# Group normalisation and a two-way column scan on one core: input loaded in channel blocks, statistics in five batches, the first scan slot split, part of the normalising on GpSimd

## The reference

```python
def ref(feature, conv_w, conv_b, prelu_a):
    Wc = conv_w[:, :, 0, 4]                      # 512 x 512
    def step(prev, x_i):
        y = einsum('oc,nch->noh', Wc, prev) + conv_b
        y = where(y >= 0, y, prelu_a * y)
        cur = y + x_i
        return (cur, cur)
    x = moveaxis(feature, 3, 0)
    _, fwd_rest = scan(step, x[0], x[1:])
    fl = concatenate([x[0:1], fwd_rest])
    _, bwd_rest = scan(step, fl[-1], fl[:-1], reverse=True)
    return moveaxis(concatenate([bwd_rest, fl[-1:]]), 0, 3)

x = x + ref(group_norm(x, G=32, eps=1e-5), ...)
```

## Time and profile before

| | before |
|---|---|
| median of 3 executions | 389.98 us |
| profiled execution, its span | 390.33 us, 388.6 us |
| TensorE busy in the span | 352.3 us (91%) |
| VectorE, ScalarE, GpSimd busy | 295.7, 224.3, 5.1 us |
| mean granted TensorE clock | 0.996 |
| HBM read, written | 13.63 MB, 12.58 MB |

### The profile page before, as it was taken

One profiled execution on the slowest core, in us unless ns is written; L12 is line 12 of the kernel. 1 busy time (PEld: TensorE's weight loads), 2 busy tenths in 40 slices (PEclk: granted clock), 3 DMA queues, 4 the chain that ended last, 5 costly groups with the idle time before them and its releaser, 6 DMA issues.

```text
span 388.6 us, 10101 instructions
## 1 busy us (share of the span) xinstructions
PE 352.3 (91%) x3080; PEld 351.0 (90%) x3080; DVE 295.7 (76%) x963; ACT 224.3 (58%) x799; POOL 5.1 (1%) x11
## 2 busy tenths in 40 slices
PE   0117799999999999999999999999999999999994
PEld 0117799999999999999999999999999999999994
DVE  2899599999765666566566788878888888888785
ACT  2663066566466566556656655665665566556554
POOL 1011100000000000000000000000000000000000
PEclk9999899999999999999999999999999999999999
DMA  7997000000000000000000112222221222222222
GB/s 248 428 422 307 2 0 1 0 0 1 0 0 0 0 0 0 0 0 0 0 0 0 56 54 81 81 69 66 81 81 55 80 81 72 63 81 81 59 76 82
DMA packets 28231, 26.30 MB, mean 68 GB/s; under 512 B 1344, under 2 KB 25920, under 8 KB 26816
## 3 DMA queue, kind: packets, MB, share of 16 engines
q1 hardware_dynamic: 27936, 26.22, 19.9%
q10 hardware_dynamic: 288, 0.00, 0.0%
HBM read 13.63 MB, written 12.58 MB: 67 GB/s over the span
## 4 chain that ended last, share of the span: by engine, by line
PE 73%; DVE 14%; DMA 6%; issue 4%; SPq 1%; ACT 1%; POOLq 0%; POOL 0%; DVEq 0%
PE psum L196 73%; DVE state L284 6%; DMA xio<-in_x 6%; DVE state L328 4%; DVE state L323 2%; DVE bstat L254 1%; SPq L158 1%; ACT above L237 0%; POOLq L41 0%; POOL rstd L387 0%; DVE xio L340 0%; ACT below L239 0%; DVE chan L264 0%; DVEq L105 0%; DVE var_eps L281 0%
## 5 line engine op out<-in xcount | busy, mean ns | idle before, releaser
L196 PE MATMUL psum<-state,w_t 128*128 (+1 forms) x3008 | 339.3, 276 | 2.8 <-DVE state L284 2.4
L196 PEld LDWEIGHTS psum<-state,w_t 128*128 128x128 f32 x3008 | 338.5, 193 | 3.4 <-DVE state L284 2.5
L237 ACT ACTIVATE above<-psum,bias 128x128 f32<-128x128 f32 x376 | 139.9, 372 | 144.4 <-PE psum L196 144.4
L323 DVE TENSOR_TENSOR state<-above,state 128x128 f32 (+1 forms) x376 | 107.5, 288 | 68.5 <-ACT above L237 66.8
L239 ACT ACTIVATE below<-psum,neg_bias 128x128 f32<-128x128 f32 x376 | 140.2, 373 | 0.0
L328 DVE SCALAR_TENSOR_TENSOR state<-below,neg_slope,state 128x128 f32 (+1 forms) x376 | 123.4, 349 | 6.7
L340 DVE TENSOR_TENSOR xio<-xio,state (+1 forms) x48 | 33.2, 692 | 1.7
L284 DVE TENSOR_SCALAR state<-xio,mean,rstd 128x352 f32<-128x352 f32 (+3 forms) x84 | 30.9, 434 | 1.2 <-POOL rstd L387 1.2
L254 DVE BATCH_NORM_STATS2 bstat<-xio 128x6 f32<-128x512 f32 (+2 forms) x45 | 23.6, 584 | 8.5 <-DMA xio<-in_x 8.4
L176 PE MATMUL psum<-chan,same_group 128*128 128x4 f32 x8 | 2.0, 322 | 25.1 <-DVE chan L264 25.1
L176 PEld LDWEIGHTS psum<-chan,same_group 128*128 128x128 f32 x8 | 1.8, 280 | 25.3 <-issue 14.7
(11 more groups left out here) (17 smaller groups left out, 8.3 us busy)
## 6 DMA issues: line engine op xcount, KB each, us to landing
out_y<-xio SPq DMA_DIRECT2D x48, 256.0 KB, 2.6
xio<-in_x SPq DMA_DIRECT2D x11, 1024.0 KB, 16.2
w_t<-in_w SPq DMA_DIRECT2D x4, 256.0 KB, 19.2
xio<-in_x SPq DMA_DIRECT2D x1, 512.0 KB, 26.4
xio<-in_x SPq DMA_DIRECT2D x2, 256.0 KB, 23.5
bias<-in_bias ACTq DMA_DIRECT2D x1, 2.0 KB, 5.1
slope<-in_slope ACTq DMA_DIRECT2D x1, 0.5 KB, 8.6
```

The lines of the kernel that those rows point to most:

```text
L196: mm = nc.tensor.matmul(psum[:, 4 * par + o, 0:COLS], w_t[:, k, o * P:(o + 1) * P], xs[k], start=k == 0, stop=k == 3)
L237: nc.scalar.activation(above[:, par, o, :], z, ACT.Relu, bias=bias[:, o:o + 1], scale=1.0).then_inc(above_done, 1)
L323: nc.vector.tensor_tensor(sts[o], above[:, par, o, :], sts[o], ALU.add).then_inc(part_done, 1)
```

## The change

- **Input and statistics.** The input is laid out and loaded as 16 blocks b = 4k + n of one channel tile and one image (`xin`, 768 KB, 6 KB in a row for each partition); block 0 comes as three pieces and block 15 as 16, 16, 8, 4 and 4 columns, so there are 22 loads. Statistics are per block, with one of three 16-column units on ScalarE in 12 of the blocks. The batches are now tile 0, tile 1, tile 2, tile 3 for images 0 to 2, and tile 3 for image 3.
- **Slot 0** is taken out of the loop and split: its four k = 0 units (`FIRST_A`) stand between the last batch's mean and its second variance matmul, the other 12 (`FIRST_B`) behind it. Each of tiles 0 to 2 waits only for GpSimd's early steps, tile 3 for `first_done`. Tile 0 is now complete after the seventh unit of `FIRST_B`. There are 12 warm-up matmuls instead of 24, once block 14 has come, and the means of the fourth batch stand behind these.
- **Normalising.** For tiles 0 to 2 the first 8 columns are done by GpSimd in chunks of 4 columns (512 elements), a subtraction and a multiplication each. VectorE does tile 3 (image by image) and later pieces of 10 columns: 2 ahead, and 2 after each of slots 0 to 30, which are unrolled.
- **Output.** `add_input` adds the input into the state in place, without its wait; column 0 has its input added before the backward half. Columns 47 to 1 are stored from the state (256 KB, 2 KB in a row for each partition), and column 0 in four stores of 64 KB, one for each tile, which stand on SyncE's queue behind the store of column 1.
- Bias and slope come in one load and are negated in one instruction.

```diff
-PIECES = [[16, 16, 16], [16, 16, 16], [16, 16, 16], [16, 16, 8, 4, 4]]
-EARLY = 4
-LATER = 11
-AHEAD = 8
-PER_STEP = 4
-WARM_UP = 24
+FIRST_A = [(0, 0), (0, 1), (0, 2), (0, 3)]
+FIRST_B = [(1, 0), (1, 1), (1, 2), (1, 3), (2, 0), (2, 1), (3, 0), (3, 1), (2, 2), (3, 2), (2, 3), (3, 3)]
+FIRST_PIECES = [16, 16, 16]
+LAST_PIECES = [16, 16, 8, 4, 4]
+BATCHES = [(0, 0, 4), (1, 0, 4), (2, 0, 4), (3, 0, 3), (3, 3, 4)]
+EARLY = 8
+CHUNK = 4
+LATER = 10
+PER_STEP = 2
+WARM_UP = 12
...
-            for i in range(W):
+            for i in range(FWD):
                 step = W - 1 - i
                 sp.wait_ge(out_ready, i + 1)
-                sp.dma_start(out[:, :, step, :, :], xio[:, :, step, :, :]).then_inc(stored, 16)
-            sp.wait_ge(stored, 16 * W)
+                sp.dma_start(out[step], state[:, step, :, :]).then_inc(stored, 16)
+            for o in range(KT):
+                sp.wait_ge(state_ready, 4 * (STEPS - 1) + o + 1)
+                sp.dma_start(out[0, :, o, :], state[:, 0, o, :]).then_inc(stored, 16)
+            sp.wait_ge(stored, 16 * (FWD + KT))
...
+            for t in range(len(BATCHES) - 1):
+                if t == len(BATCHES) - 2:
+                    pe.wait_ge(x_loaded[NBLK - 2][0], 16)
                     for _ in range(WARM_UP):
                         nc.tensor.matmul(psum[:, 5, 0:P], same_group[:, :], same_group[:, :], start=True, stop=True)
+                group_means(t)
+                group_variances(t)
+            last = len(BATCHES) - 1
+            group_means(last)
+            first_units(FIRST_A)
+            group_variances(last)
+            first_units(FIRST_B)
...
+            b = NBLK - 1
+            unit_stats(b, 0)
+            channel_stats(b - 1).then_inc(chan_done, 1)
+            unit_stats(b, 1)
+            deviations(3)
+            unit_stats(b, 2)
+            variances(3)
+            unit_stats(b, 3)
+            unit_stats(b, 4).then_inc(stats_done, 1)
+            channel_stats(b).then_inc(chan_done, 1)
+            deviations(4)
+            dve.wait_ge(mean_kept, 4)
+            dve.wait_ge(rstd_done, 4)
+            normalise(0, 3, 0, EARLY)
+            variances(4)
+            normalise(1, 3, 0, EARLY)
+            normalise(2, 3, 0, EARLY)
+            dve.wait_ge(mean_kept, 5)
+            dve.wait_ge(rstd_done, 5)
+            normalise(3, 3, 0, 2).then_inc(first_done, 1)
+            normalise(3, 3, 2, EARLY).then_inc(norm_done, 1)
...
+            def add_input(step):
+                place = ready(dve, state_step(dve, step))
+                return nc.vector.tensor_tensor(place, place, ready(dve, xin_step(dve, step)), ALU.add)
             def slot_out(j, par):
                 slot(False)(j, par)
-                add_input(j, target(j, False)).then_inc(out_ready, 1)
+                add_input(source(j, False)).then_inc(out_ready, 1)
+            add_input(0).then_inc(input_added, 1)
+            dve.wait_ge(input_added, 1)
             loop(dve, FWD, STEPS, slot_out)
...
+            for t, (k, n0, n1) in enumerate(BATCHES):
+                pool.wait_ge(var_done, t + 1)
+                nc.gpsimd.tensor_tensor(rstd[:, k, n0:n1], var_eps[:, k, n0:n1], minus_half[:, n0:n1],
                                         ALU.pow).then_inc(rstd_done, 1)
+                if k == KT - 1:
+                    continue
+                for c in range(EARLY // CHUNK):
+                    nc.gpsimd.tensor_tensor(to, xin[:, k, :, steps, :].rearrange("p n w h -> p w n h"), means,
+                                            ALU.subtract).then_inc(centred, 1)
+                for c in range(EARLY // CHUNK):
+                    pool.wait_ge(centred, t * (EARLY // CHUNK) + c + 1)
+                    nc.gpsimd.tensor_tensor(to, to, rstds, ALU.mult).then_inc(early_done, 1)
```

More of the change, by code:

```diff
@@ L135, in loop, with units, record, x_part @@
                 body(j, j % 2)
-        def starts(n):
-            return [sum(PIECES[n][:i]) for i in range(len(PIECES[n]))]
-        def x_piece(n, i, k):
-            w0 = starts(n)[i]
-            return xio[:, n, w0:w0 + PIECES[n][i], k, :]
-        def by_act(n, i, k):
-            return k == BY_ACT and PIECES[n][i] == 16
-        def records(n, k, i):
-            return sum(1 if by_act(n, q, k) else 2 for q in range(i))
+        def units(b):
+            if b == NBLK - 1:
+                sizes, by_act = LAST_PIECES, None
+            else:
+                sizes, by_act = [UNIT] * 3, 1 if b == 0 else None if b % N == N - 1 else 2
+            ends = [sum(sizes[:i + 1]) for i in range(len(sizes))]
+            whole = len(pieces(b)) == 1
+            return [(e - s, e, 0 if whole else i, i == by_act) for i, (s, e) in enumerate(zip(sizes, ends))]
+        def record(b, i):
+            return sum(1 if by_act else 2 for _, _, _, by_act in units(b)[:i])
+        def x_part(b, w0, w1):
+            return xin[:, b // N, b % N, w0:w1, :].rearrange("p w h -> p (w h)")
+        act_blocks = [b for b in range(NBLK) if any(u[3] for u in units(b))]
         block = ctx.enter_context(nc.Block())
@@ L154, in _ @@
         def _(sp):
-            for n in range(N):
-                for i, w0 in enumerate(starts(n)):
-                    steps = slice(w0, w0 + PIECES[n][i])
-                    sp.dma_start(xio[:, n, steps, :, :], x[:, n, steps, :, :]).then_inc(x_loaded[n][i], 16)
+            for b in range(NBLK):
+                w0 = 0
+                for i, size in enumerate(pieces(b)):
+                    sp.dma_start(xin[:, b // N, b % N, w0:w0 + size, :],
+                                 x[b // N, b % N, :, w0:w0 + size, :]).then_inc(x_loaded[b][i], 16)
+                    w0 += size
@@ L305, in _ @@
-            deviations(N - 1)
-            variance(N - 1)
-            dve.wait_ge(mean_kept, N)
-            dve.wait_ge(rstd_done, N)
-            for k in range(KT):
-                last = normalise(N - 1, k, 0, 1)
-            last.then_inc(first_done, 1)
-            for k in range(KT):
-                last = normalise(N - 1, k, 1, EARLY)
-            last.then_inc(norm_done, 1)
+            dve.wait_ge(counts_set, 2)
+            for b in range(NBLK - 1):
+                block_stats(b)
+                if b % N != 0:
+                    channel_stats(b - 1)
+                if b % N == N - 1:
+                    channel_stats(b).then_inc(chan_done, 1)
+                if b >= N and b % N == 0:
+                    deviations(b // N - 1)
+                if b >= N and b % N == 1:
+                    variances(b // N - 1)
@@ L333, in slot @@
                 return body
-            def add_input(j, step):
-                place = ready(dve, xio_step(dve, step))
-                result = ready(dve, state_step(dve, step))
-                dve.wait_ge(state_ready, reg(dve, j * 4 + 4, 1, 4 * STEPS))
-                return nc.vector.tensor_tensor(place, place, result, ALU.add)
-            later = [(n, k, w0, w0 + LATER) for w0 in range(EARLY, W, LATER) for n in range(N) for k in range(KT)]
+            later = [(n, k, w0, w0 + LATER) for w0 in range(EARLY, W, LATER) for k in range(KT) for n in range(N)]
             assert (W - EARLY) % LATER == 0
-            beside = -(-(len(later) - AHEAD) // PER_STEP)
+            ahead = PER_STEP
+            beside = -(-(len(later) - ahead) // PER_STEP)
             def normalise_more(first, last):
```

269 lines of the change are left out of this document (135 added, 134 removed).

## The result

| | before | after |
|---|---|---|
| median, lowest, highest | 390.05, 389.96, 390.55 us (5 runs) | 387.43, 387.28, 388.59 us (5 runs) |
| ratio of the times | | 0.9932, 95% interval 0.9918 to 0.9945 |
| profiled execution, its span | 390.33, 388.6 us | 387.43, 385.7 us |
| lead, up to slot 1's first tile on ScalarE | 51.42 us | 49.29 us |
| from there to slot 93's first tile | 330.64 us | 328.97 us |

The kernel became faster by 0.7%, where 385.6 us and 1.1% were forecast. The last three lines of the table are the three stages of the prediction; they went by -2.1, -1.7 and +0.9 us, in sum -2.9, which is the difference of the spans. Forecast were -3.7, -1.9 and +1.3.

The account below looks back on a forecast made before the run. TensorE's scan matmuls bind: slots of 3.573 us, about 279 us, can't move. Lead -3.7, slots 1 to 14 -1.9 and end +1.3 sum to -4.3: profiled 390.33 to 386.0, median 385.6 us, range 383.9 to 387.8.

Parts of the forecast that it names:

- the three stages of the prediction: Lead up to slot 1's first tile, -3.7 us; slots 1 to 14, -1.9; end of the kernel, +1.3.
- The warm-up's end, W: In the lead: block 14 lands at 32.7, 24 warm-up records take 4.8 us, so the warm-up ends at 37.5.
- The early rate: Input stream in 5.5 to 9, 241 GB/s before: might mend with one load; none counted, 0.6 us in the range.
- From W to tile 3: Lead behind the warm-up: fifth mean 2.05 us after its end, tile 3's first unit at 44.3, slot 0's first tile 44.55.
- Clock: TensorE in the lead: falls to 1.2 GHz in FIRST_A for some 3 us; rival that it stays up, 385.0, chance 0.17.
- Slot 0 to slot 1: From slot 0's first tile at 44.55 to slot 1's at 47.7, with nine units of 2.01 us behind state 0.
- Slots 1 to 14: Slot periods there return to 3.573 us and the loop's entry cost goes: 51.92 to 50.02, -1.9 us.
- GpSimd: Early normalising of tiles 0 to 2: 1.3 us per 512-element instruction, hidden; rival too slow, 393.7, chance 0.06.
- Conflict: Last power on GpSimd beside VectorE's normalises of images 1 and 2: 0.25 us taken, between 0 and 0.68.
- The larger one, with the squared deviations: Fourth batch's squared deviations on VectorE wait for GpSimd's last early multiplication: +1.2 us, in a rival of chance 0.17.
- End: Final stores on SyncE: last issue +1.75 to +2.1 us later, landing 0.5 sooner, in all +1.3 (+0.8 to +1.9).
- two rivals that did not occur: GpSimd and VectorE hold each other up, 387.2, chance 0.17; slot periods stay at 3.66, 387.5, chance 0.09.

Follow-up runs that it names:

- experiment 1: Changed kernel with 4 warm-up matmuls instead of 12: median 385.40 us, 2.0 shorter.
- experiment 3: Changed kernel with the weight loads held until block 14 has landed: median 386.85 us, 0.6 shorter.
- experiment 4: Changed kernel with the input's source laid out partition by partition, as before the change: median 388.24 us.
- experiment 5: Changed kernel with blocks 2 to 13 loaded two by two, 16 loads instead of 22: median 388.33 us.
- Experiment 9: Kernel before with 2 instead of 4 normalising pieces after a slot and 10 instead of 8 ahead: median 388.83 us against 390.18.
- experiment 2: Changed kernel with column 0 stored by one 256 KB store queued ahead of column 1's: median 385.75 us, 1.7 shorter.
- experiment 12: Changed kernel with no warm-up and column 0 stored by one store ahead of column 1's: median 385.34 us, 0.9867 of the kernel before.
- experiment 8: Changed kernel with VectorE's normalises of images 1 and 2 moved behind the last power: median 387.57 us.
- experiment 6: Changed kernel with slot 0 undivided behind the last normalise, as before the change: median 390.13 us, 2.7 longer.
- experiment 10: Kernel before with 12 instead of 24 warm-up matmuls: median 389.63 us against 390.18.
- experiment 7: Changed kernel with each of GpSimd's subtractions issued three times: median 393.54 us, 6.1 longer.

## Why the prediction was right, and where it was off

- **Bound and stages.** Right: slots run at 3.573 us before and after, and all differences lie in the three stages.
- **The warm-up's end, W.** 37.5 forecast, 38.53 measured. This is the first of two steps that failed, and the larger. The landing of block 14 was carried over from the kernel before's stream (32.7) and was 33.6, 0.9 us of the 1.0; 24 records took 4.93 us where I took 4.8. What W was said to do held: VectorE stood still for 2.71 us, and experiment 1 gives 2.0 us back by shortening the warm-up. The landing varies by 2.5 us from trace to trace in this layout, which the steady 32.1 of the kernel before gave no sign of.
- **The early rate.** Taken at nothing, with 0.6 us in the range. It rose from 241 to 391 GB/s in 5.5 to 9, and after 10 us 2.94 million bytes were in instead of 2.53, worth about 1 us. Block 14 got nothing of it: the larger lag behind the stream (2.1 us instead of 0.8, experiments 3 to 5) took more than that, and the prediction had no term for such a lag.
- **From W to tile 3.** The fifth mean started 2.16 us behind W (2.05 forecast). From there slot 0's first tile came 5.06 us later (5.00). The fourth deviations at W + 0.39 and eps at W + 1.22 are on the forecast. TensorE at half clock, not the power, was what tile 3 waited for, as worked out.
- **Clock.** Right in kind and length for this trace: down in FIRST_A, up 3.4 us later. The length was luck in part: with the same program on TensorE it was 6.8 us in the trace of the other source layout.
- **Slot 0 to slot 1.** 3.54 us instead of 3.15. VectorE's part 0 and state 0 were on time (1.23 against 1.1); the nine units took 2.31 instead of 2.01, because I counted units from start to start and left out the end of the last one, about 0.3. This is the second step that failed, 0.4 us. The prediction's own rows had the answer: in the kernel before the same chain, from slot 0's tile to slot 1's, took 3.57, and nothing in the change shortens it.
- **Slots 1 to 14, 0.24 short.** -1.67 instead of -1.9: the periods did as forecast, and slot 31 shows no entry cost. One period of 3.79, ending at 135.27, was not foreseen; it stands at the same slot in all eleven traces of the new layout, with 3.79 or 3.80. In the trace VectorE's `whole` of tile 0 starts there at 132.56, 0.39 us behind its `part`, with nothing else to wait for. Experiment 9 has its like at 224. An instruction fetch of one packet is in the DMA record near 133; that it is the cause is a guess.
- **GpSimd.** 1.02 us an instruction where I took 1.3, done by 38.30, hidden. The Trainium skill's 2.6 cycles an element ("GPSIMD Engine Reference", section 3.1), worked out as 1.1 us, is within a tenth of it.
- **Conflict.** 0.25 taken, 0.10 measured, and nothing of it on the path. The larger one, with the squared deviations, is real (0.57 us more for a 0.16 us instruction), but fell outside the changed kernel, because of the warm-up again.
- **End.** +0.9 instead of +1.3; the mechanism held, and experiment 2 gives it back. The terms: four issues at 0.46 us apart made 1.84 us (1.75 to 2.1 forecast); the last store lands in 1.7 instead of 2.6 us, 0.9 less where I had taken 0.5 off. Its rows are 512 bytes as before, so this is its size alone, and the input's rate was the wrong measure for it; a little more comes from an add that starts 0.1 earlier.
- **Sum.** 1.6 us of the lead's gain and 0.2 of the slots' was missed, and 0.4 won at the end. The measured 387.43 lies inside 383.9 to 387.8, near its upper end, which was set by two rivals that did not occur: that the range held is luck in that respect, since it allowed for no late block 14.

## What to carry to other kernels

Look at what is queued behind a warm-up: a chain that starts behind it inherits its length, so it should end when the next link is ready (4 matmuls beat 12 by 2 us; against none the medians differ by 0.8 us, which the times alone don't show). Filling a thin stretch of TensorE with real work can be worth more than the units it moves (2.2 to 2.7 us here against 1.0 worked out); the trace points to the clock, which came back under it. When a load's rate is carried over to another layout, ask also how far its last rows lag behind the stream. A store cut into tiles gains nothing if a whole store stands ahead of it in the same queue.

## What the runs showed of the hardware

- A VectorE instruction with two SBUF inputs waited for a running GpSimd instruction to end: 0.73 and 0.71 us instead of 0.16, twice.
- The granted clock in the records reads 1.00 from the start, also while matmuls go at half pace (6 records in a microsecond against 11); with no warm-up it reads 1.00 through the rise of the pace as well (experiment 12). From the first fall that it shows on, it agrees with the pace in the stretches shown here. The pace of starts tells the level in any case.
- The clock was at half for about 3.4 us in both kernels and in experiments 2, 3, 5, 8 and 9, and for about 6.8 us in others. In experiments 6 and 10 TensorE idled again behind the fall; in experiment 4 (the source's layout) its program was that of the changed kernel, so idling alone doesn't decide it. In experiment 7 it was 10.2 us.
- With another row size and set of loads block 14 was in at 32.1 to 34.6 us, from variant to variant, where the old layout's 11 MB came at 32.1 in all three traces. When it landed, 0.5 to 1.0 million bytes more had been moved than it and the loads before it make; in the old layout 0.35.
- Storing 256 KB in rows of 2 KB instead of 512 bytes took 0.33 instead of 0.53 us to issue and 2.0 instead of 2.6 to land. Storing 64 KB in rows of 512 bytes took 0.44 us to issue and 1.7 to land.
